# Transposes set between the products of two projections, and block matrices laid out with lane masks, in an adaptive-norm cross-attention kernel

## The reference

```
xq  = (1 + scale_q) * layernorm(x)   + bias_q        # scale, bias from silu(cond) @ Wss + bss
xkv = (1 + scale_kv) * layernorm(ctx) + bias_kv
q   = xq @ Wq + bq                                   # (16, 1024, 16 heads, 32)
k,v = split(xkv @ Wkv + bkv)                         # (16, 64, 16 heads, 32)
attn = softmax(q k^T / sqrt(32))
out  = x + (attn v) @ Wp + bp
```

## Time and profile before

| | |
|---|---|
| median of 3 runs | 1210.9 us (1210.82 to 1213.61) |
| the profiled execution | 1211.32 us |
| its span, first to last instruction | 1209.5 us |
| PE busy | 1180.0 us, 98% |
| weight loads busy | 772.5 us, 64% |
| DVE busy | 980.4 us, 81% |
| ACT busy | 703.0 us, 58% |
| POOL busy | 706.0 us, 58% |

### The profile page before, as it was taken

The page is one execution under the profiler, slowest core; times in us unless marked ns, Lnnn a source line. Parts: engine busy times, 40 slices in busy tenths (PEclk is TensorE's granted clock), DMA queues, the critical chain, the costliest instruction groups (busy, mean ns, idle before and its releaser), DMA issues.

```text
span 1209.5 us, 33685 instructions
## 1 busy us (share of the span) xinstructions
PE 1180.0 (98%) x11584; PEld 772.5 (64%) x11584; DVE 980.4 (81%) x2052; ACT 703.0 (58%) x1176; POOL 706.0 (58%) x948
## 2 busy tenths in 40 slices
PE   7799899999999999999999999999999999999997
PEld 2675666666666666666666666666666666666664
DVE  4787888888888888888888888888888888888875
ACT  1466556665656556665656565565656565565653
POOL 1553656657474756666575756666565656656434
PEclk9799999999999999999999999999999999999999
DMA  8110222332223232232323222323223222222222
GB/s 330 62 44 27 88 89 97 89 95 87 98 84 99 86 101 86 96 95 88 95 87 95 87 95 87 101 85 100 87 95 92 90 95 87 95 87 84 65 71 80
DMA packets 59866, 111.93 MB, mean 93 GB/s; under 512 B 6412, under 2 KB 6440, under 8 KB 59832
## 3 DMA queue, kind: packets, MB, share of 16 engines
q1 hardware_dynamic: 41400, 77.92, 21.2%
q10 hardware_dynamic: 18432, 33.56, 7.3%
HBM read 77.90 MB, written 33.55 MB: 92 GB/s over the span
## 4 chain that ended last, share of the span: by engine, by line
issue 46%; POOL 37%; POOLq 2%; DVE 0%; DVEq 0%
POOL xr L414 12%; POOL xh L381 7%; POOL w_lo L420 5%; POOL w_tmp L404 5%; POOL rstd L369 2%; POOL xr L390 2%; POOLq L221 2%; POOL nmv L365 2%; POOL veps L367 2%; POOL cur_sc L399 0%; POOLq L244 0%; POOLq L40 0%; POOLq L399 0%; DVE mv L812 0%; DVE oT_lo L827 0%
## 5 line engine op out<-in xcount | busy, mean ns | idle before, releaser
L553 ACT ACTIVATE q_hi<-ps_q,cur_bq 128x512 f16<-128x512 f32 x126 | 86.6, 687 | 268.0 <-PE ps_q L1113 230.6
L365 POOL TENSOR_TENSOR nmv<-mv,sign 128x2 f32<-128x2 f32 x128 | 27.0, 211 | 352.0 <-DVE mv L812 352.0
L820 DVE TENSOR_TENSOR xT_lo<-ps_t,xT_hi 128x512 f16<-128x512 f32 x128 | 88.5, 692 | 162.4 <-ACT xT_hi L494 162.4
L414 POOL TENSOR_TENSOR xr<-y,xr 128x512 f32<-128x512 f32 x128 | 163.1, 1275 | 46.1 <-ACT y L519 46.1
L390 POOL TENSOR_TENSOR xr<-xr,bp_row 128x512 f32<-128x512 f32 x128 | 163.1, 1274 | 13.1 <-POOL rstd L369 6.9
L876 DVE TENSOR_TENSOR pt_lo<-ps_t,pt_hi 128x512 f16<-128x512 f32 x256 | 164.7, 685 | 3.7 <-ACT pt_hi L543 3.5
L868 DVE TENSOR_TENSOR pr<-ps_s,mx 128x512 f32<-128x512 f32 x256 | 163.7, 681 | 0.0
L856 DVE TENSOR_REDUCE mx<-ps_s 128x8 f32<-128x512 f32 x256 | 158.8, 662 | 0.1
L494 ACT CAST xT_hi<-ps_t 128x512 f16<-128x512 f32 x128 | 75.0, 586 | 142.2 <-PE ps_t L1096 142.0
L584 ACT ACTIVATE pr<-pr,exp_scale 128x1024 f32<-128x1024 f32 x128 | 149.6, 1169 | 6.2 <-DVE pr L868 6.2
L543 ACT CAST pt_hi<-ps_t 128x512 f16<-128x512 f32 x256 | 136.3, 588 | 5.3 <-PE ps_t L1149 5.3
(11 more groups left out here) (160 smaller groups left out, 2323.7 us busy)
## 6 DMA issues: line engine op xcount, KB each, us to landing
x_in<-in_x_dram SPq DMA_DIRECT2D x128, 256.0 KB, 2.6
xr<-in_x_dram SPq DMA_DIRECT2D x128, 256.0 KB, 2.6
out_dram<-xr ACTq DMA_DIRECT2D x128, 256.0 KB, 2.2
raw<-in_L_xcond_Wss_kv_dram SPq DMA_DIRECT2D x4, 512.0 KB, 5.4
cx<-in_ctx_dram SPq DMA_DIRECT2D x1, 2048.0 KB, 12.4
raw<-in_L_xcond_Wss_q_dram SPq DMA_DIRECT2D x4, 512.0 KB, 13.4
raw<-in_L_xcond_Wkv_dram SPq DMA_DIRECT2D x2, 1024.0 KB, 15.7
wq<-in_L_xcond_Wq_dram SPq DMA_DIRECT2D x1, 1024.0 KB, 16.9
```

Source lines behind the costliest of these rows:

```text
L414: pool.tensor_tensor(xr[:, s, :], y[:, off % 2, :], xr[:, s, :], ALU.add).then_inc(y_ready, 1)
```

## The change

Four edits. First, PE issues each of p's eight transposes behind one product of the query projection (behind products 1 to 8 of 0 to 11), and in the output projection x's four transposes behind products 2 to 5 and o's four behind products 6 to 9. The waits stay at the first part of each group. Second, DVE does `turned_p` ahead of `softmax_shift`; its `turned_x` is written at the end of the step before and not at the start of the step, the same place. ACT does p's copies ahead of the query's, and x's copy of unit i+8 behind the query's and ahead of the exponential. Third, in step 7 `key_blocks` moves behind x's copy, ahead of the exponential. Fourth, keys and values are laid out by two ACTIVATEs each over all 128 lanes with a per-lane scale of 1 or 0 (`k_mask`, `v_mask`); the masks are row sums over the identity, two reductions on DVE at the start, and kb isn't zeroed any more.

```diff
+        k_mask = sb("k_mask", [P, 2], F32)
+        v_mask = sb("v_mask", [P, 2], F32)
...
-            pool.memset(kb[:, :, :, :, :], 0.0).then_inc(bd_ready, 1)
...
                 wait(act, s_mm, PER * b)
-                for r in range(HPG):
-                    rows = slice(DH * r, DH * (r + 1))
-                    act.copy(kb[rows, :, :, r % 2, :], k16[rows, b, :, :, :]).then_inc(kb_done, 1)
+                for r in range(2):
+                    act.activation(kb[:, :, :, r, :], k16[:, b, :, :, :], ACT.Copy, scale=k_mask[:, r:r + 1])\
+                       .then_inc(kb_done, 1)
...
                 wait(act, pv_mm, 2 * PER * b)
-                for part in range(2):
-                    for par in range(2):
-                        rows = slice(LKV * par, LKV * (par + 1))
-                        act.copy(vb[rows, part, :, par, 0:DH], v_all[rows, part, b, :, :]).then_inc(vb_done, 1)
+                for par in range(2):
+                    act.activation(vb[:, :, :, par, 0:DH], v_all[:, :, b, :, :], ACT.Copy, scale=v_mask[:, par:par + 1])\
+                       .then_inc(vb_done, 1)
...
             def step(b, i):          # ACT
-                if not (isinstance(b, int) and b == 0 and i == 0):
-                    turned_x(b, i + 7)
                 turned_o(b, i - 3)
                 output(b, i - 4)
...
                 if i == 4:
                     query_bias(b + 1)
+                turned_p(b, i - 1, 0)
+                turned_p(b, i - 1, 1)
+                query(b, i + 4)
+                turned_x(b, i + 8)
                 if i == 7:
                     key_blocks(b + 1)
-                query(b, i + 4)
-                turned_p(b, i - 1, 0)
-                turned_p(b, i - 1, 1)
                 if exists(b, i):
...
+            dve.tensor_reduce(k_mask[:, :], ident[:].rearrange("p (a j n) -> p j a n", j=2, n=DH), AX_XY, ALU.add)\
+               .then_inc(masks_ready, 1)
+            dve.tensor_reduce(v_mask[:, :], ident[:].rearrange("p (j n) -> p j n", j=2), AX_X, ALU.add)\
+               .then_inc(masks_ready, 1)
             dve.wait_ge(ld_ctx, 16)
...
             def step(b, i):          # DVE
-                if not (isinstance(b, int) and b == 0 and i == 0):
-                    turned_x(b, i + 7)
                 stats(b, i + 8)
...
                 normalise_o(b, i - 2)
-                softmax_shift(b, i)
                 turned_p(b, i - 1, 0)
                 turned_p(b, i - 1, 1)
+                softmax_shift(b, i)
                 query(b, i + 4)
+                turned_x(b, i + 8)
...
+            def turn_x_part(b, off, k):
+
+                if not exists(b, off):
+                    return
+                if k == 0:
+                    wait(pe, xh_ready, upto(b, off))
+                    wait(pe, xT_done, unit(b, off))
+                    wait(pe, pt_done, 2 * unit(b, off - 9) + 1)
+                last = pe.transpose(ps_t[:, 0, P * k:P * (k + 1)], xh[:, off % 2, P * k:P * (k + 1)], ident[:, :])
+                if k == KC - 1:
+                    last.then_inc(xT_turned, 1)
...
             def step(b, i):          # PE
                 score(b, i)
-                project(b, i + 4)
-                turn_p(b, i - 1)
-                project_out(b, i - 3)
-                turn_x(b, i + 8)
-                turn_o(b, i - 2)
+                for n in range(TERMS):
+                    project_part(b, i + 4, n)
+                    if 1 <= n < 1 + PAIRS:
+                        turn_p_part(b, i - 1, n - 1)
+                for n in range(TERMS):
+                    project_out_part(b, i - 3, n)
+                    if 2 <= n < 2 + KC:
+                        turn_x_part(b, i + 8, n - 2)
+                    if 2 + KC <= n < 2 + 2 * KC:
+                        turn_o_part(b, i - 2, n - 2 - KC)
                 weigh(b, i - 1)
```

More of the change, by code:

```diff
@@ L1095, in turn_x, with project_part @@
+            def turn_x(b, off):
                 for k in range(KC):
-                    last = pe.transpose(ps_t[:, 0, P * k:P * (k + 1)], xh[:, off % 2, P * k:P * (k + 1)], ident[:, :])
-                last.then_inc(xT_turned, 1)
-            def project(b, off, bank=ps_q, spare=0):
+                    turn_x_part(b, off, k)
+            def project_part(b, off, n, bank=ps_q, spare=0):
                 if not exists(b, off):
                     return
[L1103 to L1113, removed]
-                                         stop=(n == 3 * KC - 1))
-                        n += 1
-                last.then_inc(q_mm, 1)
+                s, m, k = (off // 4) % 2, off % 4, n % KC
+                if n == 0:
+                    if m == 0:
+                        wait(pe, xT_done, upto(b, off + 3))
+                    if off % PER < 4:
+                        wait(pe, w_done, KC * (b + off // PER) + m + 1)
+                    wait(pe, q_done, unit(b, off) - spare)
+                w, xt = ((w_hi, xT_hi), (w_hi, xT_lo), (w_lo, xT_hi))[n // KC]
+                last = pe.matmul(bank[:, :], w[:, k, P * m:P * (m + 1)], xt[:, s, k, :], start=(n == 0),
+                                 stop=(n == TERMS - 1))
+                if n == TERMS - 1:
+                    last.then_inc(q_mm, 1)
@@ L1125, in score @@
                 if off % PER == 0:
[L1126 removed]
+                    wait(pe, kb_done, 2 * (b + 1))
                 wait(pe, sub_done, 2 * unit(b, off))
@@ L1170, in weigh, with turn_o_part @@
                     last.then_inc(pv_mm, 1)
-            def turn_o(b, off):
+            def turn_o_part(b, off, k):
                 if not exists(b, off):
                     return
-                wait(pe, o_done, 2 * upto(b, off))
-                wait(pe, oT_done, unit(b, off))
-                wait(pe, pt_done, 2 * unit(b, off + 1) + bank_o(b, off) + 1 if exists(b, off + 1) else 2 * UNITS)
-                for k in range(KC):
-                    last = pe.transpose(ps_t[:, bank_o(b, off), P * k:P * (k + 1)],
-                                        o[:, HPG * k:HPG * (k + 1), :].rearrange("p h d -> p (h d)"), ident[:, :])
-                last.then_inc(o_turned, 1)
@@ L1183, in project_out @@
-            def project_out(b, off):
+                if k == 0:
+                    wait(pe, o_done, 2 * upto(b, off))
+                    wait(pe, oT_done, unit(b, off))
+                    wait(pe, pt_done,
+                         2 * unit(b, off + 1) + bank_o(b, off) + 1 if exists(b, off + 1) else 2 * UNITS)
+                last = pe.transpose(ps_t[:, bank_o(b, off), P * k:P * (k + 1)],
+                                    o[:, HPG * k:HPG * (k + 1), :].rearrange("p h d -> p (h d)"), ident[:, :])
@@ L1184, in project_out, with project_out_part @@
+                if k == KC - 1:
+                    last.then_inc(o_turned, 1)
+            def project_out_part(b, off, n):
                 if not exists(b, off):
                     return
-                if isinstance(b, int) and b == 0:
-                    wait(pe, wp_ready, 2)
-                wait(pe, oT_done, upto(b, off))
-                wait(pe, y_copied, unit(b, off))
-                n = 0
-                for ot, w in ((oT_hi, wp_hi), (oT_hi, wp_lo), (oT_lo, wp_hi)):
-                    for k in range(KC):
-                        last = pe.matmul(ps_o[:, :], ot[:, k, :], w[:, k, :], start=(n == 0), stop=(n == 3 * KC - 1))
-                        n += 1
@@ L1195, in project_out @@
-                last.then_inc(out_mm, 1)
+                k = n % KC
+                if n == 0:
+                    if isinstance(b, int) and b == 0:
+                        wait(pe, wp_ready, 2)
+                    wait(pe, oT_done, upto(b, off))
+                    wait(pe, y_copied, unit(b, off))
+                ot, w = ((oT_hi, wp_hi), (oT_hi, wp_lo), (oT_lo, wp_hi))[n // KC]
+                last = pe.matmul(ps_o[:, :], ot[:, k, :], w[:, k, :], start=(n == 0), stop=(n == TERMS - 1))
```

44 lines of the change are left out of this document (24 added, 20 removed).

## The result

| | before | after |
|---|---|---|
| median of 4 runs | 1211.04 us | 1217.78 us |
| lowest and highest | 1210.82, 1213.61 | 1217.46, 1220.62 |
| profiled execution | 1211.3 | 1217.9 |
| its span | 1209.5 | 1216.0 |

The account below looks back on a forecast made before the run. The prediction took PE as the bound, at 8.53 us a step. It summed 1211.3 + 21 (borders) + 0.5 (border into batch 15) + 1.7 (end) = 1234.5, against a median of 1234, range 1224 to 1243, chance 0.60.

Parts of the forecast that it names:

- Edit 1: PE's transposes set between products: each still takes 0.109 us, the step stays at 8.52, nothing gained.
- Rival A: Transposes hidden behind products: PE's step falls to 7.65 us, total 1204 (1190 to 1208); chance 0.11.
- Edit 2: New orders of ACT and DVE: in a plain step the chain of 8.23 us stays hidden under PE's 8.53.
- ring: Chain over PE, ACT, DVE and POOL from x's first transpose through exp and xh back to PE: 8.23 us.
- Edit 3: Mask blocks, key blocks moved ahead of exp: PE waits about 1.50 us at each of 14 batch borders, +21 us.
- 0.55 for the store: On ACT behind exp: 0.40 us for issuing the output store plus 0.15 for register instructions.
- 0.40 for the jump: On ACT at a batch's end: the jump back to the loop's start, between 0 and a bound from 0.71 us.
- The start: Steps 0 to 3: earlier halves of p win about 1 us until PE waits for xh; nothing, -1 to +1.
- The end: Steps from unit 124: shifts behind two pt_lo delay exp, 0.75 us more in three steps; +1.7 (0 to 4.9).
- the -0.6: In the last steps: 0.6 us gained since o's last transposes stand ahead of some products.
- B: No effect: borders absorbed if exp starts earlier or key blocks and jump cost under 0.3 us; 1211 to 1214, chance 0.15.
- C: Store's hole nearer 0.6 us, ring 8.75, PE waits for xh in every step: 1264 (1246 to 1285), chance 0.11.

Follow-up runs that it names:

- e3: The changed kernel with each output store issued as two halves of 256 columns: 1218.72 us, ratio 1.0069 to the kernel before.
- e9: The changed kernel with PE's order of before; ACT's and DVE's orders and the masks stay as changed: 1225.44 us, ratio 1.0125.
- e11: e9 with key_blocks back at its old place and DVE's old order in the last batch: 1210.09 us, ratio 0.9996.
- e6: The changed kernel with DVE's shifts ahead of pt_lo again from the last batch on, PE's new order kept: 1221.55 us, ratio 1.0089.
- e8: The changed kernel with key_blocks at its old place, POOL normalising x ahead of the residual, PE's and DVE's old orders in the last batch: 1210.51 us, ratio 0.9991.
- e2: The changed kernel with the key blocks as four 32-lane copies again, at their new place: 1237.71 us, ratio 1.0229.
- e4: The kernel before with PE's new order alone; ACT's and DVE's orders and the copies as before: 1400.76 us, ratio 1.1579.
- e5: The changed kernel with POOL normalising x ahead of the residual, behind a one-element operation that carries the waits: 1213.05 us, ratio 1.0023.
- e10: The kernel before with only the key and value blocks by masks, at their old places: 1211.06 us, ratio 1.0001.
- e7: The changed kernel with DVE's shifts ahead of pt_lo again in all steps: 1228.16 us, ratio 1.0146.

## Why the prediction was off, by its own steps

- **What bounds the kernel: right.** PE, without a gap, in 8.537 us steps.
- **Edit 1, nothing gained: right.** Rival A (1204) fell with the first pair of distances. Against the forecast stood a rule of the Trainium skill ("TensorE: Matmul & The Clock Gate", "LDWEIGHTS (loading the stationary operand)" and "Back-to-back issue gap"), from which the prediction worked out, as an estimate, that a transpose behind a product would take some 56 ns instead of 107: the trace after disagrees in each step, at 0.11. The Trainium skill's section on the gap gives its 56 ns for a matmul by itself and about 81 ns for a stream of load and matmul pairs, which the prediction left out; 0.11 is neither.
- **Edit 2, the plain step: right in its result, by a ring that was too long.** No hole; p's transposes, x's and o's stand where they were put, to 0.02 us. Its ring had one wait too few: oT_hi starts when the last output product is done (the 0.15 above). And there is more room than the 0.30 forecast. From exp to oT_hi are 1.30 us, and 1.04 is enough (the border); xh ends 0.72 ahead of its transpose, and 0.15 is enough. That is 0.8 us of slack: the ring through exp is 8.94 less the key blocks' 1.24, 7.7 us, where 8.23 was forecast.
- **Edit 3, the border: right in place, kind and number, wrong in size.** This step failed: 1.50 us a border forecast, 0.36 measured, 14 times, so 5.0 in place of 21. The term that was mis-sized is exp to oT_hi: 1.17 + 0.55 for the store + 0.40 for the jump = 2.12 forecast, 1.04 measured, so 1.08 of the 1.14. The rest is made of smaller differences: the key blocks at 1.24 instead of 1.40 and step 7 at 8.62 instead of 8.53 make the hole smaller, mv to xh at 3.53 instead of 3.46 and xh to PE at 0.15 instead of 0.05 larger. The 0.40 between 576.75 and 577.15 was read as time that the store takes from ACT's computing. It was a store that waited. POOL's sum, the line before which no store can leave, in the timeline of the kernel before:

```profile
575.37 1.28 POOL L414 TENSOR_TENSOR xr<-y,xr 128x512 f32<-128x512 f32 x1
```

It ends at 576.65, and the store has 576.81. Over the whole loop of before, the store follows the end of this sum by 0.16 to 0.17 us, while its distance to the end of exp goes from 0.00 to 0.25. The trace before even had a row in which the store didn't have to wait, in the last steps, next to a line of the earlier trace rows:

```profile
1176.99 0.34 ACTq L588 DMA_DIRECT2D out_dram<-xr  x1
```

exp starts at 1176.98 there and computes for 1.15 us, so this store goes out beside it. Whoever reads a DMA issue behind an ACTIVATE as its price must first ask what released it. After the change the sum is done early, and the store and the loop's jump go by while ACT still computes. e3 shows that for the store; for the jump no experiment was run, and it rests on the border's 1.04, in which no room is left.
- **The start: in the range.** -1 to +1 us was forecast, from a gain of 1.0 that is lost in step 3. The step times 0 to 3 were 5.44, 8.71, 8.19, 8.54 and are 5.43, 7.74, 8.13, 9.63: steps 0 to 2 are 1.0 shorter, and in step 3 PE waits for xh. But 0.4 of the 1.0 is before's stretch at 1.2 GHz; at one clock the gain is about 0.6 and the sum of the four steps a loss of about 0.5. The gain doesn't need PE's new order: e9 and e11 have it with the old one.
- **The end: +1.7 and 0.5 forecast, +3.1 measured.** The border into batch 15 costs nothing, where 0.5 was forecast. Late steps of 6.8 were forecast, and they are 6.77 (two of them, the third is 5.94 instead of 6.06). ACT there (answers to the earlier trace rows):

```profile
1182.31 1.15 ACT L586 ACTIVATE pr<-pr,exp_scale 128x1024 f32<-128x1024 f32 x1 [2.43 <-DVE pr L875]
...
1183.83 0.69 ACT L523 ACTIVATE y<-ps_o,y_unscale 128x512 f32<-128x512 f32 x1
1189.08 1.15 ACT L586 ACTIVATE pr<-pr,exp_scale 128x1024 f32<-128x1024 f32 x1 [2.43 <-DVE pr L875]
1190.13 0.57 ACT L506 CAST oT_hi<-ps_t 128x512 f16<-128x512 f32 x1
1190.60 0.69 ACT L523 ACTIVATE y<-ps_o,y_unscale 128x512 f32<-128x512 f32 x1
```

exp waits for the shifts 2.43 us, not 1.39. The term that failed here is the -0.6, forecast because o's transposes stand ahead of products: from the last scores to the end of the span it is +1.8 (24.5 to 26.3). The earlier transposes bring nothing, because oT_hi stands behind exp in ACT's order and exp waits for the shifts. The last scores start at 1189.77 in after, and oT_hi, above, 0.37 behind them; before they start at 1185.04, and oT_hi stood ahead of them:

```profile
1184.42 0.59 ACT L502 CAST oT_hi<-ps_t 128x512 f16<-128x512 f32 x1 [0.22 <-PE ps_t L1179]
```

That is 1.0 of the 1.8; 0.7 is one more turn of the same ring behind it, and 0.1 lies in the rest. Whose order makes the end long: with PE's old order it is DVE's (e9 has about 3.6 us of it, e11, with DVE's old order in the last batch, none); with PE's new order DVE's old one is worse still (e6, +5.0), so both must go back (e8).
- **The sum with measured terms:** 1211.3 + 5.2 + 3.1 - 1.8 = 1217.8, and the profiled run had 1217.9 (three parts of the same two spans, so this is no test). The forecast was 1211.3 + 21 + 0.5 + 1.7.
- **Rivals.** B (the borders are absorbed) named half of the right doubt: the jump costs nothing that shows, but the key blocks alone cost 1.24 and not under 0.3, and exp starts as long after x's copy as was read (0.49). What neither B nor the forecast had is that ACT goes on 1.04 after exp's start. A hole was left, and the time lies between B's range and mine. C (the ring binds everywhere, over a store's hole of 0.6) is dead by the plain step and e3. Two waits stood in no case: the next scores for the key blocks (e2, e9), and bank 0 in each step when PE's order goes alone (e4, weighed only when e4 was planned).

## What to carry to other kernels

- Here a full engine gained nothing from a new order of its instructions. It could have gained only if one of them got cheaper beside its neighbour, and two distances in the trace of before answered that. What the new order changed is who waits at the borders, the start and the end, and those are where to look for a loss; where the other engines' orders are not moved with it, it is in each step (e4).
- Work moved into a chain that has 0.8 us of slack must be priced there. The key blocks cost nothing at their old place, at 2.54 or at 1.24 us; at the new place the short form costs 5 us in all and the long form 24.5 (e2).
- An interval behind an instruction is a price only if nothing released it. Look for a row without a wait in other stages of the same trace (here the last steps, 1176.99), and take the bound of zero in earnest where there is none.
- Before a difference between two traces is put down to a change, compare their granted clocks over the same stretch: 3.4 us at 1.2 GHz were worth about 0.4 us in before's steps 0 to 3 (an estimate) and 1.6 us in e9's end.

## What the runs showed of the hardware

- A DMA issue on ACT's queue goes out while an ACTIVATE of ACT before it in the program still waits or computes (646.13, exp 646.33), and two a step cost no time (e3).
- An ACTIVATE with a scale for each lane took 0.72 on 128x512 f16. The view by lines:

```profile
L514 ACT ACTIVATE kb<-k,k_mask 128x512 f16 (+1 forms) x32 | 21.3, 717 | 0.0
```

Two of them take 1.24 from the first start to exp's start, 0.62 each, and a copy of 32 lanes with as many elements per lane takes 0.64 (2.54 for four). Four times the lanes and a scale cost nothing here, and the saving was in the number of instructions.
- At the borders the waits view named pt_lo, and the chip had waited for xh (e5). The half of pt_lo that the transpose needs was done 0.93 us before it, and a later update of the same semaphore lay closer. Look up in the timeline when the awaited update came; the proof is to move one of the two.
- The granted clock fell to 1.2 GHz for 3.4 us, while PE was busy again, at most 1.5 us behind a wait of PE: of 2.20 us (before, 124.7), 2.28 us (e10, 131.9), 2.90 us (e7, 135.3) and 1.95 us (e9, 1208.6). It did not fall behind waits of 2.07 and 2.28 us in e4 (122.4, 130.4). So the length of the last wait doesn't tell which execution pays.
